# Head attention scores: three fp32r products on 64x128 tiles in place of fp32 products on 64x64 tiles

## The reference

```python
q = jnp.einsum('bsd,hpd->bhsp', x, q_w) + q_b          # 16 heads of 64
k = jnp.einsum('bsd,hpd->bhsp', x, k_w) + k_b
v = jnp.einsum('bsd,hpd->bhsp', x, v_w) + v_b
scores = jnp.einsum('bhqp,bhkp->bhqk', q, k) / jnp.sqrt(jnp.float32(P))
attn = jax.nn.softmax(scores, axis=2)                  # over the queries
ctx = jnp.einsum('bhqk,bhkp->bqhp', attn, v)
out = concat @ l_w.T + l_b
```

## Time and profile before

| | |
|---|---|
| median of 3 runs | 1458.87 us (1458.61 to 1458.96) |
| the profiled execution | 1458.3 us, span 1456.6 us |
| TensorE busy, share of the span | 1424.7 us, 98% |
| VectorE | 1069.7 us, 73% |
| ScalarE | 918.2 us, 63% |
| GpSimd | 279.7 us, 19% |
| granted TensorE clock, mean | 0.999 of full speed |

### The profile page before, as it was taken

The page is one execution under the profiler, slowest core; times in us unless marked ns, Lnnn a source line. Parts: engine busy times, 40 slices in busy tenths (PEclk is TensorE's granted clock), DMA queues, the critical chain, the costliest instruction groups (busy, mean ns, idle before and its releaser), DMA issues.

```text
span 1456.6 us, 43343 instructions
## 1 busy us (share of the span) xinstructions
PE 1424.7 (98%) x18426; PEld 1023.6 (70%) x18426; DVE 1069.7 (73%) x2172; ACT 918.2 (63%) x1727; POOL 279.7 (19%) x325
## 2 busy tenths in 40 slices
PE   7999989999999999999999999999999999999997
PEld 6989954656777665667777756577777566777487
DVE  6885168987676678887666788876667887787764
ACT  5775766666666666666666666666666666666544
POOL 5166713022110022120000121300000213000046
PEclk9999999999999999999999999999999999999999
DMA  7502311011000111010000110100101111101002
GB/s 223 205 19 61 93 48 48 17 29 47 22 19 16 35 29 32 26 44 17 16 17 16 43 31 23 44 24 16 31 16 40 31 26 34 34 16 31 2 19 59
DMA packets 44464, 58.30 MB, mean 40 GB/s; under 512 B 8231, under 2 KB 32656, under 8 KB 44144
## 3 DMA queue, kind: packets, MB, share of 16 engines
q1 hardware_dynamic: 35120, 38.27, 9.5%
q0 software_dynamic: 9152, 17.26, 4.4%
HBM read 22.14 MB, written 19.32 MB: 28 GB/s over the span
## 4 chain that ended last, share of the span: by engine, by line
PE 87%; DVE 5%; issue 3%; POOL 2%; ACT 2%; DMA 1%; POOLq 0%; DVEq 0%; ACTq 0%
PE bank L1134 30%; PE bank L1147 29%; PE bank L1057 6%; PE bank L1062 4%; PE bank L1071 3%; PE bank L1289 2%; PE bank L1285 2%; PE bank L1246 1%; PE bank L406 1%; PE bank L434 1%; DVE stats L1330 1%; PE bank L811 1%; PE bank L815 1%; PE bank L803 1%; POOL xslots L651 1%
## 5 line engine op out<-in xcount | busy, mean ns | idle before, releaser
L1178 ACT ACTIVATE prob<-bank,nmx 128x1024 f32<-128x1024 f32 x512 | 570.3, 1114 | 418.2 <-DVE nmx L1169 416.8
L1169 DVE TENSOR_REDUCE nmx<-bank 128x1 f32<-128x1024 f32 x512 | 626.4, 1224 | 202.3 <-PE bank L1134 183.7
L1147 PE MATMUL bank<-prob,vsc 64*64 64x512 f32 x4096 | 644.3, 590 | 1.4 <-DVE ctxT L1196 0.7
L1134 PE MATMUL bank<-q,k 64*64 64x512 f32 x2048 | 526.9, 592 | 3.0 <-ACT prob L1178 1.9
L1134 PE MATMUL bank<-q,ks 64*64 64x512 f32 x2048 | 525.5, 590 | 0.0
L1147 PEld LDWEIGHTS bank<-prob,vsc 64*64 64x64 f32 x4096 | 240.7, 133 | 116.1 <-issue 41.5
L1057 PE MATMUL bank<-xT,wqkv_sb 64*64 64x256 f32 (+1 forms) x1560 | 213.0, 435 | 0.0
L1134 PEld LDWEIGHTS bank<-q,ks 64*64 64x64 f32 x2048 | 138.3, 133 | 77.9 <-issue 18.5
L1741 POOL DMA_INDIRECT yg<-yslots,row_ring x64 | 64.6, 1010 | 604.6 <-PE bank L1134 579.2
L1134 PEld LDWEIGHTS bank<-q,k 64*64 64x64 f32 x2048 | 134.3, 133 | 32.3 <-ACT prob L1178 7.4
L1057 PEld LDWEIGHTS bank<-xT,wqkv_sb 64*64 64x64 f32 x1560 | 93.5, 133 | 86.5 <-issue 34.4
(11 more groups left out here) (270 smaller groups left out, 1596.0 us busy)
## 6 DMA issues: line engine op xcount, KB each, us to landing
ks<-k SPq DMA_DIRECT2D x62, 256.0 KB, 3.1
yslots<-slots_sb SPq DMA_DIRECT2D x7, 640.0 KB, 3.6
slots_sb<-xslots SPq DMA_DIRECT2D x5, 640.0 KB, 4.6
xslots<-xhat_r POOLq DMA_DIRECT2D x5, 512.0 KB, 7.1
yslots<-xhat_r POOLq DMA_DIRECT2D x5, 512.0 KB, 12.3
w_sb<-in_w SPq DMA_DIRECT2D x1, 2048.0 KB, 9.3
wqkv_sb<-in_wqkv SPq DMA_DIRECT2D x1, 2048.0 KB, 18.8
xslots<-xhat_r,row_s POOLq DMA_INDIRECT x112
```

The lines of the kernel that those rows point to most:

```text
L1134: ins = nc.tensor.matmul(bank[rows(c), SC[h][n], :], kk[r, cols(2 * j + c, HD)], qst[pi % 2][r, cols(n, HALF)], start=True, stop=True)
L1147: ins = nc.tensor.matmul(bank[rows(h), CX[n], :], vsc[s][rows(r), rows(h)], prob[g % 3][h][rows(r), cols(n, HALF)], start=(j == 0 and firs ...
L1169: nc.vector.tensor_reduce(nmx[:, 2 * s + h:2 * s + h + 1], bank[:, SC[h][0]:SC[h][0] + 2, :], mybir.AxisListType.XY, ALU.max, negate=True) ...
L1178: nc.scalar.activation(prob[g % 3][h][:].rearrange("p (n c) -> p n c", c=HALF), bank[:, SC[h][0]:SC[h][0] + 2, :], ACT.Exp, bias=nmx[:, 2 ...
```

## The change

The scores become three products per head and query half: rounded k with rounded q, rounded k with the rest of q, and the rest of k with rounded q, all fp32r, summed in PSUM. Each is 64 rows x 128 columns with 512 queries, on either half of the array's rows; there are no column tiles any more. q and k are copied out of PSUM by ScalarE into two shared buffers (`qk`) and split from there: for the first pair by VectorE, else by GpSimd (a copy to fp32r and a subtraction, L1785 and L1787 being their like). k_hi, k_lo and their swapped copies have one buffer for all pairs, q_hi and q_lo two. The swap takes four DMAs per half of the keys, at j = 2 and j = 6. The order in which the quarters of q and k are projected changes (`QK_PART`). GpSimd's gathers and scatters are written step by step so that the splits can stand between them, and the gathers of batch row 2 use `yg` as the others do (`yg2` goes). Context, projection, output and chunks stay 64x64.

```diff
-        def score_part(pe, g, h, half):
+        def scores(pe, g, h):
             pi, j = g // T, g % T
-            if half == 0 and j == 0:
+            if j == 0:
                 if h == 0:
-                    pe.wait_ge(c_hi, 4 * (pi + 1))
-                if pi == 0:
-                    pe.wait_ge(c_first[h], 16)
-                else:
-                    pe.wait_ge(c_dup[h], 16 * pi)
-            if half == 0 and g == T // 2:
-                pe.wait_ge(c_second[h], 16)
-            if half == 0 and g > 0:
+                    pe.wait_ge(c_split, 4 * pi + 3)
+                pe.wait_ge(c_dup[h], 32 * (pi + 1))
+                if g == 0 and h == 1:
+                    pe.wait_ge(c_hi, 4)
+            if j == T // 2:
+                if h == 0:
+                    pe.wait_ge(c_split, 4 * pi + 4)
+                pe.wait_ge(c_dup2[h], 32 * (pi + 1))
+            if g > 0:
                 pe.wait_ge(c_exp, 2 * g + h - 1)
-            r, n = rows(half), (h + half) % 2
-            kk = (kst2 if n else kst)[pi % 2]
-            for c in range(2):
-                ins = nc.tensor.matmul(bank[rows(c), SC[h][n], :], kk[r, cols(2 * j + c, HD)], qst[pi % 2][r, cols(n, HALF)],
-                                       start=True, stop=True)
-            if half == 1:
-                ins.then_inc(c_qk, 1)
-
-        def scores(pe, g, h):
-            for half in range(2):
-                score_part(pe, g, h, half)
+            for m, (k, ks, q) in enumerate(((k_hi, ks_hi, q_hi), (k_hi, ks_hi, q_lo), (k_lo, ks_lo, q_hi))):
+                for half in range(2):
+                    r, n = rows(half), (h + half) % 2
+                    ins = nc.tensor.matmul(bank[:, SC[h][n], :], (ks if n else k)[r, cols(j)], q[pi % 2][r, cols(n, HALF)],
+                                           start=(m == 0), stop=(m == 2))
+            ins.then_inc(c_qk, 1)
...
         def qk_evac(a, pi, k, src):
...
+            if n > 1:
+                a.wait_ge(c_split, n - 1)
             a.wait_ge(c_proj, 6 * pi + k + 1)
...
+        def split_gpsimd(p, pi, k):
+
+            n = 4 * pi + k
+            hi, lo = short_parts(pi, k)
+            full = qk[n % 2][:]
+            p.wait_ge(c_hi, n + 1)
+            if k == 0:
+                p.wait_ge(c_qk, 2 * (T * (pi - 1) + T // 2))
+            elif k == 3:
+                p.wait_ge(c_qk, 2 * T * pi)
+            nc.gpsimd.tensor_copy(hi, full).then_inc(c_short, 1)
+            p.wait_ge(c_short, n + 1)
+            nc.gpsimd.tensor_tensor(lo, full, hi.bitcast(F32), ALU.subtract).then_inc(c_split, 1)
...
-            for h in range(2):
-                score_max(v, 0, h)
+            for k in range(3):
+                split_vector(v, k)
+            score_max(v, 0, 0)
+            split_vector(v, 3)
+            score_max(v, 0, 1)
...
-        def k_swap(sp, pi):
-
-            hold(sp, c_hi, 4 * pi + 2)
-            for h in range(2):
-                sp.dma_start(kst2[pi % 2][rows(1 - h), :], kst[pi % 2][rows(h), :]).then_inc(c_dup[h], 16)
+        def k_swap(sp, pi, half):
+
+            c = cols(half, HALF)
+            hold(sp, c_split, 4 * pi + (4 if half else 1))
+            for h in range(2):
+                for dst, src in ((ks_hi, k_hi), (ks_lo, k_lo)):
+                    sp.dma_start(dst[rows(1 - h), c].bitcast(F32), src[rows(h), c].bitcast(F32)).then_inc((c_dup2 if half else c_dup)[h], 16)
...
+        SPLIT_AT = {2: 0, 3: 1, 4: 2, 6: 3}
 
         def c_gpsimd(p):
-            first_gather(p, 1)
-            for b in range(B - 1):
-                c_scatter(p, b)
-                if b == 0:
-                    first_gather(p, 2)
-                c_gather(p, b + 1, range(2))
-            c_scatter(p, B - 1)
+            for g in range(LAST + 1):
+                pi, j = g // T, g % T
+                transfers_gpsimd(p, g, 0)
+                if j in SPLIT_AT and pi < NPAIRS - 1:
+                    split_gpsimd(p, pi + 1, SPLIT_AT[j])
+                transfers_gpsimd(p, g, 1)
```

More of the change, by code:

```diff
@@ L1026, in project @@
             if k < 4:
-                c = (WK, WK, WQ, WQ2)[k]
+                c, half = QK_PART[k]
                 for h in range(2):
-                    ins = nc.tensor.matmul(bank[rows(h), bk, :], wqkv_sb[:, row, c + h * HD:c + (h + 1) * HD], xT_c[:, cols(k % 2, HALF)],
+                    ins = nc.tensor.matmul(bank[rows(h), bk, :], wqkv_sb[:, row, c + h * HD:c + (h + 1) * HD], xT_c[:, cols(half, HALF)],
                                            start=True, stop=True)
@@ L1057, in project_piece @@
                     ins = nc.tensor.matmul(bank[rows(h), PJ[0] + t, 0:n], wqkv_sb[rows(r), row, c + h * HD:c + (h + 1) * HD],
-                                           xT_c[rows(r), k % 2 * HALF + t * n:k % 2 * HALF + (t + 1) * n], start=first, stop=not first)
+                                           xT_c[rows(r), half * HALF + t * n:half * HALF + (t + 1) * n], start=first, stop=not first)
                 return ins
@@ L1663, in store_third @@
                          xres[:, (B - 2) * T + 4 * h:(B - 2) * T + 4 * h + 4, :]).then_inc(stored, 16)
-        def first_swap(sp):
-            for half, done in enumerate((c_first, c_second)):
-                hold(sp, c_hi, 1 + half)
-                for h in range(2):
-                    sp.dma_start(kst2[0][rows(1 - h), cols(half, HALF)], kst[0][rows(h), cols(half, HALF)]).then_inc(done[h], 16)
         def c_sync(sp):
-            first_swap(sp)
+            for half in range(2):
+                k_swap(sp, 0, half)
             store_slots(sp, 3, 2)
@@ L1746, in c_scatter @@
-        def c_scatter(p, b):
-            hold(p, g_idx, b + 1)
-            for k in range(2):
-                for t in range(T):
-                    c = k * T + t
-                    paced(p, b * STEPS + 22 + c // 2, c % 2)
-                    nc.gpsimd.indirect_dma_start(out=xslots[:, :], out_offset=bass.IndirectOffsetOnAxis(ap=row_s[:, k, t:t + 1], axis=0),
-                                                 in_=xhat_r[:, t, :], in_offset=None,
-                                                 bounds_check=B * SLOTS - 1, oob_is_err=False).then_inc(g_sc, 16)
@@ new lines, in last_gather, with c_scatter @@
+        def last_gather(p):
+            c_gather_ready(p, B)
+            for c in range(2 * T):
+                if c % 2 == 0:
+                    beside_last(p, c // 2)
+                c_gather(p, B, c)
+        def c_scatter(p, g, c, h):
+            paced(p, g, h)
+            k, t = divmod(c, T)
+            nc.gpsimd.indirect_dma_start(out=xslots[:, :], out_offset=bass.IndirectOffsetOnAxis(ap=row_s[:, k, t:t + 1], axis=0),
+                                         in_=xhat_r[:, t, :], in_offset=None,
+                                         bounds_check=B * SLOTS - 1, oob_is_err=False).then_inc(g_sc, 16)
@@ L2054, in _ @@
             owners_gpsimd(p, step)
-            c_gather(p, B, range(2))
+            last_gather(p)
         @block.scalar
```

102 lines of the change are left out of this document (61 added, 41 removed).

## The result

The changed kernel takes **1584.4 us** (median of 4 runs, 1583.1 to 1586.1) against 1458.7 us (median of 4, 1456.6 to 1459.0): it is slower, by a ratio of 1.087 [1.085, 1.089]. The forecast was 1573 us with a range of 1490 to 1620. The profiled execution took 1586.1 us with a span of 1584.4 us, at a mean granted clock of 0.998 of full speed (0.999 before).

What follows compares the result with a forecast made beforehand. The prediction took TensorE's chain of matmuls, 4.29 us an ordinary step, as the bound. Its terms, -85 + 173 + 20 + 4 + 2 = +114 us on the profiled 1458.3 us, gave 1572.3, as a median 1573 us; range 1490 to 1620.

Steps and rivals of the forecast that it cites:

- What bounds the kernel: Ordinary attention steps: the chain of waits runs through TensorE's matmuls alone, 4.29 us a step.
- the loop of 3.73 us: Scores, maximum, exponent, next scores: a step can't fall below 3.73 us; ordinary steps lie 0.56 us above.
- Products: 512 score calls: three fp32r products at 0.231 us, 0.69 a call in place of 0.86; 85 us gained.
- Rival B: Score products: the two row groups take turns, 355 us more, 1928 us; chance 0.04.
- Switches of the tile shape: Four shape changes a step between 64x64 and 64x128, with open weight loads: 0.68 us a step, 173 us lost.
- Rival A: Four borders of a step: shape switches with equal row groups are free, 1380 us; chance 0.11.
- Row groups forced level: First block of 31 pairs, context alone on row group 0: 31 x 0.66 = 20 us lost, bounds 0 and 27.
- Splits on GpSimd: 124 casts and subtractions, hidden except where they hold VectorE's `scale_v`: 4 us lost, bounds 0 and 62.
- DMAs: k's swap as 8 transfers a pair in place of 2, halves needed about four steps later: nothing lost.
- Prologue: Before the first scores: three splits on VectorE in series, 2 us lost, bounds 0 and 5.

Runs made afterwards that it cites:

- e2: Changed kernel with the scores of both heads issued together in every step, then both context halves: 1494.8 us, ratio 1.025 to the kernel before.
- e4: Changed kernel without the third product (rest of k with rounded q): 1480.2 us, ratio 1.015 to the kernel before.
- e5: Kernel before, with only the order changed: scores of both heads, then both context halves, in every step: 1520.3 us against 1487.5, ratio 1.022.
- e3: Kernel before with one fp32 64x128 score matmul in place of two of 64x64, no splits: 1663.1 us, ratio 1.141.
- e7: Changed kernel with both heads' scores together at the first block of 31 pairs only: 1581.9 us, ratio 1.065 to the kernel before.
- e9: Kernel before with both heads' scores together at the first block of 31 pairs only: 1487.3 us against 1485.9, ratio 1.001.
- e1: Changed kernel with splits, transfers and copies kept, but scores again as fp32 64x64 tiles of rounded q and k: 1473.8 us, ratio 1.010 to the kernel before.
- e6b: Changed kernel with each GpSimd cast and subtraction done twice: 1652.4 us, against 1613.2 for the unedited changed kernel on the same chip.

## Why the prediction was right, point by point

From profile to profile the time rose by 1586.1 - 1458.3 = 127.8 us; the forecast's sum was 114.

- **What bounds the kernel: right.** The chain stayed on TensorE and the loop of 3.73 us stayed below it. e2, e4 and e5 show that there is less room than its 0.56 us: as soon as TensorE's step falls to about 4.3 us in another order or 4.2 in the same one, some steps are set by VectorE. The forecast's 3.73 is a floor for steps with nothing beside them, not for all.
- **Products: -85 forecast, -84 measured.** The row groups run beside each other, each product at 0.231 us, as the rows of the last routing gave it. e4 took one product away and the median step fell by 2 x 0.231. Rival B is out.
- **Switches of the tile shape: +173 forecast, 254 x 0.71 = +180 measured.** By terms: way into 64x128, pause 0.110 (forecast 0.095; 0.09 if counted from the last of the four tiles) and open load 0.104 (0.10); way out, pause 0.092 (0.095) and open load 0.048 (0.05). e3 shows the same borders with no other part of the change. Rival A, with free borders for equal row counts, is out: it needed less than 0.33 us a step. This agrees with the Trainium skill (TensorEngine Tiling (Array Packing), Tiling Modes, Key Properties), which calls 64x64 and 64x128 two modes and says that changing modes drains TensorE; the 0.09 to 0.11 us is this case's number for it.
- **Row groups forced level: +20 forecast, +20 measured at the first blocks, and 3 more in other steps.** The 31 first blocks rose by 1.05 us each, the others by 0.41 on average: 31 x 0.64 = 20. e7, which takes this and one border away, gained 1.13 us in each of these steps, of which 1.13 - 0.355 = 0.77 are this term. The size was in part luck: the forecast took 0.2 us off as what the kernel before already loses there to the lone context, and e9 does not bear that out. The forecast also left out 22 other steps, 18 of them with a piece of the mixture of experts beside them (L1246). They rose by 0.13 to 0.25 us more than the ordinary ones, 3.3 us together. The same steps do so by the same 3.3 us in e3, which has borders and no splits; so this comes with the borders and is no cost of GpSimd's. The end of one such step, before and after:

```profile
339.44 0.60 PE L1134 MATMUL bank<-q,k 64*64 64x512 f32 x2
339.49 0.39 PE L1062 MATMUL bank<-wqkv_sb,xT 64*64 64x128 f32 x4
```

```profile
356.98 0.39 PE L1065 MATMUL bank<-wqkv_sb,xT 64*64 64x128 f32 x4
357.30 0.49 PE L1169 MATMUL bank<-q_hi,k_hi 64*128 64x512 f32 x1
```

  In the kernel before, the next scores start on one row group while the other still has matmuls of the step; in the changed kernel they wait. I take this for the cause, but it isn't shown: other steps end in the same way and rise no more than the ordinary ones.
- **Splits on GpSimd: +4 forecast; about +2.5 measured on the path, and the place was only half right.** The forecast named `scale_v`. It is held 50 times, for 22 us in all. But all VectorE instructions of the stage together last some 50 us beyond their usual durations (each one less the median of its kind, summed), against 2 before, and most of that is small side work. In the timeline of the changed kernel:

```profile
595.12 1.29 POOL L1143 TENSOR_TENSOR q_lo<-qk,q_hi 128x512 fp32r<-128x512 f32 x1
595.30 1.12 DVE L1378 TENSOR_TENSOR newton<-rstd 128x8 f32<-128x8 f32 x1
599.43 0.50 PE L1169 MATMUL bank<-q_hi,k_hi 64*128 64x512 f32 x1 [0.36 <-ACT prob L1208]
```

  The hold of 0.95 us (1.12 in place of 0.17) reaches TensorE as a wait of 0.36 us, and mostly not at all. Apart from the first blocks and the 22 steps above, 8 steps of the stage lie more than 0.05 us above the usual rise, 2.5 us together, and in 7 of them TensorE waits for an exponent. So the term is nearly as forecast, but not by its sum, in which 62 x 0.1 would be 6 and not 4. The Trainium skill's rule (SBUF — State Buffer, Who interferes with whom), that such instructions lock each other out for their whole length, agrees with the rows (595.12 + 1.29 = 596.41, and the held instruction ends at 596.42). Yet the forecast was right not to take its upper bound of 62, for a held instruction costs nothing while the step has room. This room came from the borders: splits, transfers and copies together cost 12.9 us in e1, whose steps are 4.3 us, and a second set of splits 39 us in e6b. So the term depends on the step's length and on how much GpSimd has to do, and can't be added to the others as a constant.
- **DMAs: 0 forecast; right in the stage, wrong ahead of it.** In the stage TensorE waits for no transfer. Before the first two scores it waits 2.57 and 0.30 us for the transfer of k's rest, and this is what sets the prologue.
- **Prologue: +2 forecast, +4 measured, by another path.** The first scores of the third block start at 209.67 in place of 205.86. The forecast took three splits in series; they end at 199.32. The chain of waits of the changed kernel goes from the first of them, done at 197.21, over four transfers that SP issues one behind the other, 0.6 us apart, to the second head's scores:

```profile
199.17 2.47 DMA ks_lo<-k_lo
...
201.69 1.54 PE bank L1169 x6
```

  The last transfer lands at 201.64, 2.3 us behind the last of the three splits. TensorE stood idle meanwhile, and then its granted clock fell to the lower of its two levels (1.2 GHz), from 201.8 to 205.2 us. A stretch of it (length, busy PE, PEld, DVE, ACT, POOL, then the clock):

```profile
203.10:205.00 1.90, 1.90 (x20) 1.84 (x20) 1.74 (x2) 0.91 (x3) 0.00 (x0) 0.50 0.03 9
```

  In it 32 projection matmuls take 2.96 us, where the kernel before takes 1.97 at a granted clock of 1.00. Half speed for 3.4 us is about 1.7 us of the 4. e1 has the same prologue, wait and clock, and its 4.1 us.

By these sizes -84 + 180 + 23 + 2.5 + 4 = +125.5. Two more entries bring it to 127.8. Five steps with nothing beside them, four of them in the last pair, rose less than the rest, since in the kernel before the loop already held them (four of them at 3.73 to 3.75 us, where TensorE's work is 4 x 0.86 = 3.44): -1.7. And an ordinary step rose by 0.393 us where the terms above give 0.382, which makes 3 us over 253 steps; the rest, 1 us, is rounding. Of the 14 us by which the forecast was low, 7 are the borders (the way into 64x128, above all), 3 the 22 steps, 3 the ordinary steps' remainder, 2 the prologue and 1 the products; the splits and the last pair took 3 of them back.

## What to carry to other kernels

Count what stands between the matmuls, not only the matmuls: here each change of the tile shape and back cost 0.355 us, as much as one and a half products of 512 columns, so a change of shape pays only where at least that is saved between two borders. Look for such pauses in the distance between starts, since a busy share of 98% was the same with and without 180 us of them. And price a lock between two engines by the room of the step that it falls in: the splits cost about 2.5 us in steps of 4.7 us, and with their transfers and copies 13 in steps of 4.3.

## What the runs showed of the hardware that I had not expected

- The pause at a change of shape is the same both ways, 0.09 us, counted from the last tile that starts; counted from the first it looks longer from 64x64 to 64x128 (0.110), since the four tiles start over 0.02 us.
- With a change of shape behind it, a context on one row group alone costs its full length: the 31 first blocks rose by 0.64 us each beyond the others. In 22 other steps the borders cost 0.13 to 0.25 us more than in the rest.
- The first fp32 matmul with a 128-wide load behind a border costs 0.105 us more than its columns (e3), the same as the fp32r one (0.104); a 64-wide load costs 0.048.
- GpSimd's subtraction of 1.29 us holds even VectorE operations of 128x8, which then last 1.13 us in place of 0.17.
- Two chips differ by 29 us with the same kernel, 26 of them outside the attention stage; the ratio of changed to unchanged kernel was 1.087 on both.
